# Expert weights relaid in device memory and fetched by GpSimd only where the expert changes

## The chip, the cores and the metric

The kernel runs on one core of a Trainium2 chip. The metric is the time of one execution on the device, in microseconds (us). The core has five engines that run side by side and meet at semaphores: TensorE (PE in the profile; its weight loads are PEld), VectorE (DVE), ScalarE (ACT), GpSimd (POOL) and SyncE (SP), which here only issues DMAs. Sixteen DMA engines move data between device memory and the on-chip memory of 128 partitions. A difference of less than about 0.2% can't be told from none.

## The reference

Two layers over a graph of 2,500 nodes with 1,024 features and 40,000 edges. Each layer is a graph convolution followed by a feed-forward block, both added to `x`. The part that matters here is the last block, a mixture of eight experts of which each node uses two:

```python
router_probs = softmax(flat @ router_w + router_b)          # [2500, 8]
topk_probs, topk_idx = top_k(router_probs, 2)
h1 = gelu(einsum('td,edh->teh', flat, rw1) + rb1)           # rw1: [8, 1024, 256]
expert_out = einsum('teh,ehd->ted', h1, rw2) + rb2          # rw2: [8, 256, 1024]
mixed = einsum('ted,te->td', expert_out, weights)           # weights: top 2 only
```

Before it stands the second graph layer, with attention: every edge gets a score from its two nodes, and rows of the projected nodes are summed with those scores.

## The kernel before

The program is a row of stages, each with its own block of five instruction streams; a stage starts when the one before has ended on all engines. The stages that the change touches are three.

**Attention** (`stage_attention`, about 1428 to 2050 us). SP loads the weight matrix W in eight pieces of 512 KB (line 1032). TensorE computes the scores of all nodes; when they are all kept, SP stores the source half as rows in device memory (line 1034, 40 KB, `el`). GpSimd then gathers a row per edge, 352 DMAs of 128 rows (line 1051), while TensorE computes the projected rows. TensorE has 160 products to do before it needs the first 32 gathers (`Z_FIRST`); from then on the order of products and score chunks is written out by `attention_turns`. All of SP's DMAs go through one queue, in order.

**Routing** (`stage_route`, about 3052 to 3106 us). The 5,000 places (2,500 nodes, two experts each) are sorted by expert into 28 groups of 256 (`PG`), each group with one expert. Each expert's part is padded to whole groups, and groups past the end get the last expert. `group_expert` holds the expert of each group.

**Experts** (`stage_experts`, about 3106 to 3580 us). For each group SP reads the group's expert into a register and loads the two weight matrices, 1 MB each, into one buffer each (`raw1`, `raw2`, both `e_raw` in the profile; lines 1978 and 1981), as soon as VectorE has freed it. ScalarE casts them to a high part (`e_w_hi`), VectorE subtracts to get the low part (`e_w_lo`) and frees the buffer. GpSimd gathers the 256 rows of the group in two DMAs (line 1995), TensorE turns them (`e_turned`), ScalarE and VectorE split them (`e_hi`, `e_lo`), TensorE computes the hidden layer in 48 products (`e_hidden`), ScalarE the Gelu (`e_act_out`), VectorE splits it (`e_h_hi`, `e_h_lo`), TensorE computes the output in 24 products (`e_y`), VectorE adds the bias, ScalarE scales, and GpSimd adds the rows to the output in device memory with two scatters (line 2005); each pair of scatters waits until the pair before has landed.

The stage is a software pipeline written out in full (`in_turn`): in step s every engine works on groups s, s-1 and s-2, in the order of its `body`. ScalarE in step s does: the two casts of turned rows of group s-1, the two casts of the weights of group s, the Gelu of group s-1, the scaling of group s-2. VectorE: `e_lo` of s-1 and output sums of s-2 in turn, the two weight subtractions of s, `e_h_hi` and `e_h_lo` of s-1. GpSimd: the gathers of s, then the scatters of s-2. ScalarE and VectorE begin the stage with a wait for all three bias loads (`small_in`), of which the last is a broadcast of 4 MB (`e_all_bias`, line 1984).

Of the kernel before, what the change touches and what calls it, by code (L numbers as in the profile page):

```python
# [6 lines left out]
I32 = mybir.dt.int32  # L7
U32 = mybir.dt.uint32
ALU = mybir.AluOpType
ACT = mybir.ActivationFunctionType  # L10
AX = mybir.AxisListType
P = 128
N_NODES = 2500
N_EDGES = 40000
D = 1024
KD = D // P
# [16 lines left out]
EXPERTS = 8  # L33
# [961 lines left out]
def stage_attention(nc, g):  # L995
    with ExitStack() as ctx:
# [19 lines left out]
        stored = [sem(f"stored{k}") for k in range(2)]  # L1016
# [12 lines left out]
        def _(sp):  # L1029
            for c in range(KD):  # L1030
                at_least(sp, w_low, c - 1)
                sp.dma_start(zout[:, c % 2, :].rearrange("p (h f) -> p h f", h=HEADS), w_rows[c]).then_inc(w_in[c % 2], 16)
            sp.wait_ge(scores_kept, NT)
# [4 lines left out]
            for k in range(2):  # L1038
                sp.wait_ge(stored[k], 16 * (NT // 2))

# [704 lines left out]
def stage_route(nc, g):  # L1745
    with ExitStack() as ctx:
# [26 lines left out]
        group_count = sb("group_count", [P, PG])  # L1773
# [13 lines left out]
        def _(pool):  # L1787
# [7 lines left out]
            q.iota(iota_g[:], pattern=[[GT * P, PG]], base=0, channel_multiplier=0, **small)  # L1795
            q.memset(ones[:], 1.0)
# [33 lines left out]
        def _(dve):  # L1830
# [99 lines left out]
            st.done(v.tensor_scalar(g.expert[:], group_count[:], float(EXPERTS - 1), None, ALU.min))  # L1930

# [13 lines left out]
def stage_experts(nc, g):  # L1945
    with ExitStack() as ctx:
# [14 lines left out]
                 "hi_ready lo_ready hidden_ready act_ready split_ready y_ready y_kept y_scaled bias1_ready").split()  # L1961
# [7 lines left out]
        def _(sp):  # L1969
# [5 lines left out]
            for i in range(PG):  # L1975
                e = sp.value_load(g.expert[0:1, i:i + 1], min_val=0, max_val=EXPERTS - 1)
                at_least(sp, m.raw1_used, i)
                sp.dma_start(raw1[:].rearrange("p (c f) -> p c f", c=KD),
                             g.rw1.rearrange("e (c p) f -> p (e c) f", p=P)[:, bass.ds(e * KD, KD), :]).then_inc(m.raw1_in, 16)
                at_least(sp, m.raw2_used, i)  # L1980
                sp.dma_start(raw2[:].rearrange("p (m n) -> p m n", m=2),
                             g.rw2.rearrange("e (m p) n -> p (e m) n", p=P)[:, bass.ds(e * 2, 2), :]).then_inc(m.raw2_in, 16)
                if i == 0:
                    sp.dma_start(all_bias2[:], g.rb2.rearrange("e d -> (e d)").partition_broadcast(P)).then_inc(m.small_in, 16)

        @block.gpsimd
        def _(pool):
            def body(item):
# [11 lines left out]
                if it:  # L2000
                    for q in range(GT):
# [5 lines left out]
                            in_=y_out[:, it.i % 2, q, :], in_offset=None, compute_op=ALU.add).then_inc(y_added, 16)  # L2007
# [198 lines left out]
```

## Time and profile before

| | us |
|---|---|
| median of three runs | 3577.93 |
| lowest, highest | 3573.08, 3578.49 |
| profiled execution, its own time | 3581.93 |
| its span | 3580.2 |
| TensorE busy over the span | 2847.5 (80%) |
| VectorE busy | 2455.1 (69%) |
| GpSimd busy | 1714.2 (48%) |
| ScalarE busy | 1536.9 (43%) |

The span is the stretch that the profiler recorded; the time of the same execution is 1.7 us longer. Busy shares are averages over stages with different limits, and a change in one stage is judged by what that stage waits for. In the profile a row of engines reads: where, engine, operation, output<-inputs, shape, how often, and in brackets the idle time before it with the instruction that ended it.

### The profile page before, as it was taken

The numbers are of one execution on the slowest core, as the hardware profiler recorded it, in microseconds if no ns is written. First come the engines' busy times: TensorE is split into PE (matmuls) and PEld (weight loads), VectorE is DVE, ScalarE is ACT, GpSimd is POOL, SyncE is SP. The second block draws the span as 40 slices with busy tenths as digits, with TensorE's granted clock in tenths as the row PEclk, the third lists the DMA queues.
The fourth block names the chain that finished last, engine by engine and source line by source line (L and its number), as shares of the span: only waits on it lengthen the run. The fifth ranks groups of instructions, "written<-read, shape, count | busy, mean of one in ns | idle before, by whom it ended". The sixth has DMA issues, their size and how long they took to land. (4 is left out here: it accounts for less than half of the span.)

```text
span 3580.2 us, 50457 instructions
## 1 busy us (share of the span) xinstructions
PE 2847.5 (80%) x13602; PEld 2228.0 (62%) x13602; DVE 2455.1 (69%) x5351; ACT 1536.9 (43%) x3068; POOL 1714.2 (48%) x1564
## 2 busy tenths in 40 slices
PE   0996102999996777889899899999999699289996
PEld 0885101444443665877777588888887688278886
DVE  6222602999997665527777799999999564467774
ACT  1221000333333765523333377777776332055554
POOL 4777873666664221247777344444443111023332
PEclk9998555999998898579999899999999688599999
DMA  3333306999997011101111188887877332289997
GB/s 103 79 96 109 92 2 246 353 349 351 348 347 225 30 41 55 40 20 20 26 20 26 38 263 259 262 261 260 260 261 230 114 139 106 103 239 284 282 284 181
DMA packets 223841, 609.09 MB, mean 170 GB/s; under 512 B 47387, under 2 KB 85650, under 8 KB 223582
## 3 DMA queue, kind: packets, MB, share of 16 engines
q0 software_dynamic: 139008, 429.63, 38.7%
q1 hardware_dynamic: 84702, 177.85, 14.5%
q8 instruction: 65, 1.06, 0.1%
q14 instruction: 66, 0.54, 0.1%
HBM read 521.91 MB, written 85.11 MB: 170 GB/s over the span
## 5 line engine op out<-in xcount | busy, mean ns | idle before, releaser
L640 POOL DMA_INDIRECT g_rows<-z_rows,edge_src x704 | 700.4, 995 | 615.6 <-PE g_totals L1397 307.8
L705 PE MATMUL g_sums<-g_rows,g_share 128*128 128x512 f32 x704 | 333.0, 595 | 211.3 <-DVE g_goes L746 211.3
L483 POOL DMA_INDIRECT edge_list<-payload,row_i x320 | 402.3, 1257 | 144.1 <-issue 141.3
L691 ACT ACTIVATE g_scaled_hi<-g_rows,edge_weight_sorted 128x1024 fp32r<-128x1024 f32 x176 | 202.6, 1151 | 540.6 <-DMA g_rows<-z_rows,edge_src 505.4
L1051 POOL DMA_INDIRECT shared<-el_rows,edge_src x352 | 334.8, 951 | 178.8 <-issue 107.0
L1390 PE MATMUL g_sums<-g_rows,g_share 128*128 128x256 f32 x1408 | 348.9, 391 | 0.0
L705 PEld LDWEIGHTS g_sums<-g_rows,g_share 128*128 128x128 f32 x704 | 133.5, 190 | 312.3 <-DVE g_goes L746 211.7
L1342 ACT ACTIVATE g_scaled_hi<-g_rows,g_factor 128x256 fp32r<-128x256 f32 x704 | 299.9, 496 | 4.3 <-DMA g_rows<-z_rows,edge_src 3.2
L1466 DVE SCALAR_TENSOR_TENSOR g_scaled_lo<-g_rows,g_factor,g_scaled_hi 128x256 fp32r<-128x256 f32 x704 | 293.4, 479 | 1.1 <-ACT g_scaled_hi L1342 0.9
L1390 PEld LDWEIGHTS g_sums<-g_rows,g_share 128*128 128x128 f32 x1408 | 255.6, 191 | 27.6
L1245 DVE TENSOR_REDUCE t_largest<-t_masked 128x4 f32<-128x512 f32 x352 | 231.9, 685 | 55.7 <-PE t_masked L1117 49.4
L728 DVE SCALAR_TENSOR_TENSOR g_scaled_lo<-g_rows,edge_weight_sorted,g_scaled_hi 128x1024 fp32r<-128x1024 f32 x176 | 225.9, 1283 | 41.5 <-ACT g_scaled_hi L691 39.6
L2005 POOL DMA_INDIRECT out_dram<-e_y_out,sorted_token x56 | 89.3, 1594 | 270.4 <-ACT e_y_out L2082 255.7
L1428 DVE TENSOR_TENSOR x_all<-x_all,g_sums 128x1024 f32 x176 | 213.9, 1216 | 0.0
L738 DVE TENSOR_TENSOR x_all<-x_all,g_sums 128x1024 f32 x176 | 213.3, 1212 | 0.4 <-PE g_sums L710 0.2
L710 PE MATMUL g_sums<-g_scaled_hi,g_goes 128*128 128x512 f32 x352 | 159.4, 453 | 33.8 <-DVE g_scaled_lo L728 33.1
L710 PEld LDWEIGHTS g_sums<-g_scaled_hi,g_goes 128*128 128x128 f32 x352 | 66.1, 188 | 172.4 <-DVE g_scaled_lo L728 163.3
L1167 ACT ACTIVATE t_apart<-iota,t_minus_place 128x128 fp32r<-128x128 f32 x352 | 125.9, 397 | 109.0 <-PE t_masked L1117 108.1
L1115 PE MATMUL t_masked<-t_never,t_apart 128*128 128x512 f32 x352 | 149.1, 423 | 23.2 <-DVE t_largest L1245 14.3
L1475 DVE TENSOR_TENSOR e_w_lo<-e_raw,e_w_hi 128x2048 fp32r<-128x2048 f32 x56 | 125.8, 2285 | 30.0 <-ACT e_w_hi L2061 28.5
L1579 POOL TENSOR_TENSOR x_all<-x_all,s_bias 128x1024 f32<-128x1024 f32 (+1 forms) x20 | 46.7, 2356 | 207.2 <-ACT s_rows L1651 207.2
L1117 PE MATMUL t_masked<-t_el_rows,t_pick 128*128 128x512 f32 x352 | 144.3, 410 | 0.0
(359 smaller groups left out, 7696.5 us busy)
## 6 DMA issues: line engine op xcount, KB each, us to landing
e_raw<-in_L_ffn_rw_dram SPq DMA_DIRECT2D x56, 1024.0 KB, 7.5
g_rows<-z_rows,edge_src POOLq DMA_INDIRECT x704, 5.7
z_rows<-z_zout SPq DMA_DIRECT2D x20, 512.0 KB, 2.9
x_rows<-x_all SPq DMA_DIRECT2D x20, 512.0 KB, 2.7
z_rows<-t_zout SPq DMA_DIRECT2D x20, 512.0 KB, 2.8
s_x<-x_rows SPq DMA_DIRECT2D x10, 1024.0 KB, 8.9
xn_rows<-s_rows SPq DMA_DIRECT2D x10, 1024.0 KB, 4.1
z_x<-in_x_dram SPq DMA_DIRECT2D x19, 512.0 KB
```

The costliest lines, as they stand in the source:

```text
L483: pool.indirect_dma_start(out=g.lists[k], out_offset=bass.IndirectOffsetOnAxis(ap=row_i[0:EP, c:c + 1], axis=0), in_=payload[0:EP, c, :], ...
L640: pool.indirect_dma_start(out=r.rows[:, slot, :], out_offset=None, in_=table, in_offset=bass.IndirectOffsetOnAxis(ap=g.src[:, i * GT + q:i ...
L705: nc.tensor.matmul(sums[:, k, h, :], share[:, k, :], r.rows[:, k * GT, h * HALF:(h + 1) * HALF], start=True, stop=False)
L710: mm = nc.tensor.matmul(sums[:, k, h, :], goes[:, k, :], part[:, m, h * HALF:(h + 1) * HALF], start=False, stop=n == 1)
L728: v.scalar_tensor_tensor(out=scaled_lo[:, m, :], in0=r.rows[:, k * GT + 1, :], scalar=g.weight[:, bass.ds(it.i * GT + 1, 1)], in1=scaled_h ...
L738: v.tensor_tensor(to, to, sums[:, it.buf(4)].rearrange("p h n -> p (h n)"), ALU.add).then_inc(added, 1)
L1051: pool.indirect_dma_start(out=g.edge_el[:, n, :], out_offset=None, in_=g.el, in_offset=bass.IndirectOffsetOnAxis(ap=g.src[:, n:n + 1], axi ...
L1245: v.tensor_reduce(largest[:, q, :], masked[:, n % 3, :].rearrange("p (h n) -> p h n", h=HEADS), AX.X, ALU.max).then_inc(taken, 1)
L1342: ins = s.activation(scaled_hi[:, m, cols], r.rows[:, k * GT + 1, cols], ACT.Copy, scale=factor[:, k, 1, h:h + 1])
L1390: t.matmul(sums[:, m, h // 2, h % 2 * HF:(h % 2 + 1) * HF], share[:, m, h, :], r.rows[:, k * GT, h * HF:(h + 1) * HF], start=False, stop=F ...
L1428: v.tensor_tensor(to, to, sums[:, m].rearrange("p h n -> p (h n)"), ALU.add).then_inc(added, 1)
L1466: ins = v.scalar_tensor_tensor(out=scaled_lo[:, m, cols], in0=r.rows[:, k * GT + 1, cols], scalar=factor[:, k, 1, h:h + 1], in1=scaled_hi[ ...
```

## The change

Two tables are added in device memory, `w1_rows` and `w2_rows`, each of 1,024 rows of 8 KB: row e*128+p holds what partition p needs of expert e, in one run. In the attention stage SP copies the sixteen matrices from the inputs into them, memory to memory, behind the loads of W and ahead of the store of the score rows. Routing computes `weight_row`, for each group and partition the row of the table, with 1,024 added where the group has the same expert as the group before: such a row is out of bounds, and the fetch leaves it out. In the expert stage the weights are fetched by GpSimd as indirect DMAs, group 0's ahead of everything and group i+1's at the end of step i, behind the gathers and scatters of that step. SP is left with the bias loads. The 4 MB bias has a semaphore of its own (`bias2_in`), for which only VectorE waits, before its first output sum. The casts and subtractions are done for every group as before.

```diff
--- before.py
+++ after.py
@@ -1013,7 +1013,7 @@
         masked, row_bank = a.psum("t_masked", [P, 3, HALF]), a.psum("t_row_bank", [P, HALF])
         w_in = [sem(f"w_in{k}") for k in range(2)]
         el_in = [sem(f"el_in{b}") for b in range(NB)]
-        stored = [sem(f"stored{k}") for k in range(2)]
+        stored, relaid = [sem(f"stored{k}") for k in range(2)], sem("relaid")
         (w_high, w_low, mv_ready, std_ready, rstd_ready, xn_ready, turned_ready, hi_ready, lo_ready, scores_ready,
          scores_kept, el_stored, apart_ready, pick_ready, parts_ready, rows_turned, rows_ready, masked_ready,
          taken, z_ready, z_kept, v_done) = (sem(n) for n in (
@@ -1030,6 +1030,11 @@
             for c in range(KD):
                 at_least(sp, w_low, c - 1)
                 sp.dma_start(zout[:, c % 2, :].rearrange("p (h f) -> p h f", h=HEADS), w_rows[c]).then_inc(w_in[c % 2], 16)
+            for e in range(EXPERTS):
+                sp.dma_start(g.w1_rows[e * P:(e + 1) * P, :].rearrange("p (c f) -> p c f", c=KD),
+                             g.rw1[e].rearrange("(c p) f -> p c f", p=P)).then_inc(relaid, 16)
+                sp.dma_start(g.w2_rows[e * P:(e + 1) * P, :].rearrange("p (m n) -> p m n", m=2),
+                             g.rw2[e].rearrange("(m p) n -> p m n", p=P)).then_inc(relaid, 16)
             sp.wait_ge(scores_kept, NT)
             sp.dma_start(g.el.rearrange("(t p) h -> p t h", p=P), g.scores[:, :, 0:HEADS]).then_inc(el_stored, 16)
             for t in range(NT):
@@ -1037,6 +1042,7 @@
                 sp.dma_start(g.z1[t * P:(t + 1) * P, :], zout[:, t % 2, :]).then_inc(stored[t % 2], 16)
             for k in range(2):
                 sp.wait_ge(stored[k], 16 * (NT // 2))
+            sp.wait_ge(relaid, 16 * 2 * EXPERTS)
 
         @block.gpsimd
         def _(pool):
@@ -1770,7 +1776,8 @@
         late, member = sb("late", [P, EXPERTS, TOPK, NEAR]), sb("member", [P, EXPERTS, NEAR])
         spare, spare_place, fits = (sb(n, [P, EXPERTS, NEAR]) for n in ("spare", "spare_place", "fits"))
         of_group = sb("of_group", [P, PG, EXPERTS])
-        group_count = sb("group_count", [P, PG])
+        group_count, row_of = sb("group_count", [P, PG]), sb("row_of", [P, PG])
+        repeats, partition = sb("repeats", [P, PG]), sb("partition", [P, 1])
         at_row, at_col = sb("at_row", [P, ALL, P], F32R), sb("at_col", [P, ALL, 3, PT], F32R)
         is_col = sb("is_col", [P, ALL, PT])
         held, empty = sb("held", [P, PT]), sb("empty", [P, PT])
@@ -1793,6 +1800,8 @@
             q.iota(iota_r[:], pattern=[[1, P]], base=0, channel_multiplier=0, **small)
             q.iota(iota_c[:], pattern=[[1, PT]], base=0, channel_multiplier=0, **small)
             q.iota(iota_g[:], pattern=[[GT * P, PG]], base=0, channel_multiplier=0, **small)
+            q.iota(partition[:], pattern=[[0, 1]], base=0, channel_multiplier=1, **small)
+            q.memset(repeats[:], 0.0)
             q.memset(ones[:], 1.0)
             q.memset(none[:], 0.0)
             q.memset(place_i[:], PT * P)
@@ -1928,6 +1937,11 @@
                                 ALU.is_equal).then_inc(rows_ready, 1)
             st.link(v.tensor_reduce(group_count[:], of_group[:], AX.X, ALU.add))
             st.done(v.tensor_scalar(g.expert[:], group_count[:], float(EXPERTS - 1), None, ALU.min))
+            st.link(v.tensor_scalar(group_count[:], group_count[:], float(EXPERTS - 1), None, ALU.min))
+            st.done(v.tensor_tensor(repeats[:, 1:PG], group_count[:, 1:PG], group_count[:, 0:PG - 1], ALU.is_equal))
+            st.link(v.tensor_scalar(row_of[:], group_count[:], float(P), partition[:, 0:1], ALU.mult, ALU.add))
+            st.done(v.scalar_tensor_tensor(out=g.weight_row[:], in0=repeats[:], scalar=float(EXPERTS * P), in1=row_of[:],
+                                           op0=ALU.mult, op1=ALU.add))
 
             dve.wait_ge(pairs_sorted, 1)
             st.link(v.tensor_copy(held[:], sorted_pairs[:, 0:PT]))
@@ -1958,7 +1972,7 @@
         turned, y = a.psum("e_turned", [P, 2, HALF]), a.psum("e_y", [P, GT, 2, HALF])
         hidden = a.psum("e_hidden", [P, HALF])
         names = ("small_in raw1_in raw2_in raw1_used raw2_used w1_high w2_high v_done turned_ready "
-                 "hi_ready lo_ready hidden_ready act_ready split_ready y_ready y_kept y_scaled bias1_ready").split()
+                 "hi_ready lo_ready hidden_ready act_ready split_ready y_ready y_kept y_scaled bias1_ready bias2_in").split()
         m = Named(**{n: a.sem(f"e_{n}") for n in names})
         gathered = [[a.sem(f"e_gathered{k}{q}") for q in range(GT)] for k in range(2)]
         y_added = a.sem("e_y_added")
@@ -1972,19 +1986,21 @@
                     sp.dma_start(all_bias1[:].rearrange("p (e m) -> p m e", m=2)[:, c, :],
                                  g.rb1.rearrange("e (m p) -> m p e", p=P)[c]).then_inc(m.small_in, 16)
 
-            for i in range(PG):
-                e = sp.value_load(g.expert[0:1, i:i + 1], min_val=0, max_val=EXPERTS - 1)
-                at_least(sp, m.raw1_used, i)
-                sp.dma_start(raw1[:].rearrange("p (c f) -> p c f", c=KD),
-                             g.rw1.rearrange("e (c p) f -> p (e c) f", p=P)[:, bass.ds(e * KD, KD), :]).then_inc(m.raw1_in, 16)
-                at_least(sp, m.raw2_used, i)
-                sp.dma_start(raw2[:].rearrange("p (m n) -> p m n", m=2),
-                             g.rw2.rearrange("e (m p) n -> p (e m) n", p=P)[:, bass.ds(e * 2, 2), :]).then_inc(m.raw2_in, 16)
-                if i == 0:
-                    sp.dma_start(all_bias2[:], g.rb2.rearrange("e d -> (e d)").partition_broadcast(P)).then_inc(m.small_in, 16)
+            sp.dma_start(all_bias2[:], g.rb2.rearrange("e d -> (e d)").partition_broadcast(P)).then_inc(m.bias2_in, 16)
 
         @block.gpsimd
         def _(pool):
+            def weights(i):
+                for raw, table, used, arrived in ((raw1, g.w1_rows, m.raw1_used, m.raw1_in),
+                                                  (raw2, g.w2_rows, m.raw2_used, m.raw2_in)):
+                    at_least(pool, used, i)
+                    pool.indirect_dma_start(
+                        out=raw[:], out_offset=None, in_=table,
+                        in_offset=bass.IndirectOffsetOnAxis(ap=g.weight_row[:, i:i + 1], axis=0),
+                        bounds_check=EXPERTS * P - 1, oob_is_err=False).then_inc(arrived, 16)
+
+            weights(0)
+
             def body(item):
                 it = item(0)
                 if it:
@@ -2005,6 +2021,9 @@
                         pool.indirect_dma_start(
                             out=g.out, out_offset=bass.IndirectOffsetOnAxis(ap=g.sorted_token[:, n:n + 1], axis=0),
                             in_=y_out[:, it.i % 2, q, :], in_offset=None, compute_op=ALU.add).then_inc(y_added, 16)
+                it = item(0)
+                if it and it.i + 1 < PG:
+                    weights(it.i + 1)
             in_turn(PG, body, 2)
             pool.wait_ge(y_added, 16 * PT)
 
@@ -2043,7 +2062,7 @@
         @block.scalar
         def _(act):
             s = nc.scalar
-            act.wait_ge(m.small_in, 48)
+            act.wait_ge(m.small_in, 32)
 
             def body(item):
                 for q in range(GT):
@@ -2087,7 +2106,6 @@
         def _(dve):
             v = nc.vector
             st = Steps(dve, m.v_done)
-            dve.wait_ge(m.small_in, 48)
 
             def body(item):
                 for q in range(GT):
@@ -2104,6 +2122,8 @@
                         if q == 0:
                             e = dve.value_load(g.expert[0:1, it.i:it.i + 1], min_val=0, max_val=EXPERTS - 1)
                             shift = all_bias2[:, bass.ds(e * D, D)]
+                        if n == 0:
+                            dve.wait_ge(m.bias2_in, 16)
                         dve.wait_ge(m.y_ready, n + 1)
                         at_least(dve, y_added, (it.i - 1) * GT * 16)
                         v.tensor_tensor(y_out[:, k, q, :], y[:, q].rearrange("p h n -> p (h n)"), shift,
@@ -2140,6 +2160,7 @@
         sw1=sw1, sb1=sb1, sw2=sw2, sb2=sb2, rw1=rw1, rb1=rb1, rw2=rw2, rb2=rb2, out=out,
         lists=[scratch(f"edge_list{k}", [P * NE, 4]) for k in range(LISTS)],
         z0=scratch("z0_rows", [NPAD, D]), z1=scratch("z1_rows", [NPAD, D]), el=scratch("el_rows", [NPAD, 4]),
+        w1_rows=scratch("w1_rows", [EXPERTS * P, KD * EH]), w2_rows=scratch("w2_rows", [EXPERTS * P, 2 * D]),
         x2=scratch("x2_rows", [NPAD, D]), xn3=scratch("xn3_rows", [NPAD, D]),
     )
     with ExitStack() as ctx:
@@ -2168,6 +2189,7 @@
         g.logits = a.sb("logits", [P, NT, EXPERTS])
         g.sorted_prob = a.sb("sorted_prob", [P, PT])
         g.expert = a.sb("group_expert", [P, PG], I32)
+        g.weight_row = a.sb("weight_row", [P, PG], I32)
         g.sorted_token = a.sb("sorted_token", [P, PT], I32)
         with nc.sbuf_tensor("x_all", [P, NT, D], F32) as x_all:
             g.x_all = x_all
```

SP's queue in the attention stage, before (W load, score rows, projected rows, end of the stage, next loads):

```order
L1028 UNCONDITIONAL_BRANCH
L1032 DMA t_zout<-in_L_gnn_W_dram 128x4x256 x8
L1034 DMA el_rows<-shared 128x20x4
L1037 DMA z_rows<-t_zout 128x1024 x20
L996 UNCONDITIONAL_BRANCH
```

and in the difference between the two programs at that place:

```order
 L1032 DMA t_zout<-in_L_gnn_W_dram 128x4x256 x8
-L1034 DMA el_rows<-shared 128x20x4
-L1037 DMA z_rows<-t_zout 128x1024 x20
+L1034 DMA w_rows<-in_L_ffn_rw_dram 1024x1x256
+L1036 DMA w_rows<-in_L_ffn_rw_dram 256x1x1024
...
+L1039 DMA el_rows<-shared 128x20x4
+L1042 DMA z_rows<-t_zout 128x1024 x20
```

The pair of `w_rows` copies stands eight times, once for each expert, and the store of the score rows comes after all sixteen.

GpSimd's stream at the start of the expert stage, before (the loop is written out, so that each step stands by itself; `e_rows` is a gather of rows, `out_dram` a scatter):

```order
L1986 UNCONDITIONAL_BRANCH
L1995 DMA e_rows<-xn_rows,sorted_token 128x1024 x6
L2005 DMA out_dram<-e_y_out,sorted_token 2500x1024 x2
L1995 DMA e_rows<-xn_rows,sorted_token 128x1024 x2
L2005 DMA out_dram<-e_y_out,sorted_token 2500x1024 x2
```

and now (`e_raw` is a fetch of weights):

```order
L1991 UNCONDITIONAL_BRANCH
L1997 DMA e_raw<-w_rows,weight_row 128x2048 x2
L2011 DMA e_rows<-xn_rows,sorted_token 128x1024 x2
L1997 DMA e_raw<-w_rows,weight_row 128x2048 x2
L2011 DMA e_rows<-xn_rows,sorted_token 128x1024 x2
L1997 DMA e_raw<-w_rows,weight_row 128x2048 x2
L2011 DMA e_rows<-xn_rows,sorted_token 128x1024 x2
L2021 DMA out_dram<-e_y_out,sorted_token 2500x1024 x2
L1997 DMA e_raw<-w_rows,weight_row 128x2048 x2
L2011 DMA e_rows<-xn_rows,sorted_token 128x1024 x2
L2021 DMA out_dram<-e_y_out,sorted_token 2500x1024 x2
```

From the fourth group on, its weights stand behind the scatters of an earlier group and ahead of its own gathers. On SP's stream the 56 weight loads and the register reads between them are gone; what is left of the stage there is this:

```order
L1504 UNCONDITIONAL_BRANCH
L1982 UNCONDITIONAL_BRANCH
L1986 DMA e_all_bias<-in_L_ffn_rb_dram 128x8x1 x2
L1989 DMA e_all_bias<-in_L_ffn_rb_dram 128x8192
L1960 UNCONDITIONAL_BRANCH
```

The bias broadcast no longer has the first group's weights ahead of it on that queue. TensorE's and ScalarE's instructions stand as before.

## Rows read from the trace of the kernel before

**Rows 1.** Chain that ended last, from 3050 us: start, length (us), what.
```profile
3109.97 21.66 DMA e_all_bias<-in_L_ffn_rb_dram
...
3143.77 7.33 PE e_hidden L253 x48
...
3346.49 1.62 POOL out_dram L2005
...
3361.37 1.61 POOL out_dram L2005
```

**Rows 2.** Waits from 3100 to 3580 us: us in total, times, longest.
```profile
PE e_y L253 <- DVE e_h_lo L1475: 34.9, 28, 2.1
```

**Rows 3.** Stretches: us, busy (x) by engine, PEclk, DMA share, GB/s.
```profile
core 0: us, PE busy (x) PEld busy (x) DVE busy (x) ACT busy (x) POOL busy (x), PEclk, DMA share, GB/s
1478.00:1553.70 75.70, 67.44 (x314) 66.32 (x315) 38.07 (x98) 32.15 (x37) 4.72 (x2) 0.50 0.03 8
...
3120.00:3126.00 6.00, 0.00 (x0) 0.00 (x0) 0.00 (x0) 0.00 (x0) 0.00 (x0) 0.50 1.09 465
...
3138.40:3141.00 2.60, 1.53 (x8) 1.56 (x8) 0.92 (x1) 0.00 (x0) 0.00 (x0) 0.50 1.05 362
...
3300.00:3520.00 220.00, 200.73 (x1295) 175.77 (x1294) 153.60 (x119) 129.30 (x135) 77.31 (x60) 1.00 0.98 283
```

**Rows 4.** ScalarE in order of time, head and one later period of the stage.
```profile
3131.66 1.90 ACT L2061 CAST e_w_hi<-e_raw 128x2048 fp32r<-128x2048 f32 x1 [76.21 <-DMA e_all_bias<-in_L_ffn_rb_dram]
...
3135.26 1.00 ACT L2054 CAST e_hi<-e_turned 128x1024 fp32r<-128x1024 f32 x1
...
3351.57 1.91 ACT L2061 CAST e_w_hi<-e_raw 128x2048 fp32r<-128x2048 f32 x1
...
3359.22 0.84 ACT L2075 ACTIVATE e_act_out<-e_hidden,e_bias 128x256 f32<-128x256 f32 x2 [3.70 <-PE e_hidden L253]
```

**Rows 5.** VectorE in order of time, the same period.
```profile
3354.60 4.49 DVE L1475 TENSOR_TENSOR e_w_lo<-e_raw,e_w_hi 128x2048 fp32r<-128x2048 f32 x2
3360.09 0.43 DVE L2127 CAST e_h_hi<-e_act_out 128x512 fp32r<-128x512 f32 x1 [1.00 <-ACT e_act_out L2075]
```

**Rows 6.** GpSimd in order of time, the same period.
```profile
3348.41 1.58 POOL L2005 DMA_INDIRECT out_dram<-e_y_out,sorted_token  x1 [0.30 <-issue]
3350.30 0.99 POOL L1995 DMA_INDIRECT e_rows<-xn_rows,sorted_token  x1 [0.30 <-issue]
3351.60 0.97 POOL L1995 DMA_INDIRECT e_rows<-xn_rows,sorted_token  x1 [0.30 <-issue]
```

**Rows 7.** SP's queue in order of time, the same period.
```profile
3342.18 0.37 SPq L1978 DMA_DIRECT2D e_raw<-in_L_ffn_rw_dram  x1
```

**Rows 8.** DMA issues of the whole trace: last number is median us to landing.
```profile
shared<-el_rows,edge_src POOLq DMA_INDIRECT x352, 2.4
...
e_rows<-xn_rows,sorted_token POOLq DMA_INDIRECT x56, 7.8
```

**Rows 9.** Tile `e_raw`: landing of its 56 loads.
```profile
DMA to landing us min/median/max: 6.0/7.5/12.4
```

**Rows 10.** SP's queue in order of time, attention stage.
```profile
1427.87 50.16 SPq L1032 DMA_DIRECT2D t_zout<-in_L_gnn_W_dram  x8
1553.67 0.37 SPq L1034 DMA_DIRECT2D el_rows<-shared  x1
```

**Rows 11.** GpSimd in order of time, attention stage.
```profile
1561.18 0.98 POOL L1051 DMA_INDIRECT shared<-el_rows,edge_src  x1 [71.82 <-DMA el_rows<-shared]
```

**Rows 12.** VectorE in order of time, attention stage and end of routing.
```profile
1602.53 0.27 DVE L1238 CAST t_el_parts<-shared 128x128 fp32r<-128x128 f32 x1 [8.66 <-DMA shared<-el_rows,edge_src]
...
3104.53 0.22 DVE L1933 COPY r_held<-r_sorted_pairs 128x56 f32<-128x56 f32 x1 [6.12 <-PE r_sorted_pairs L1825]
```

**Rows 13.** TensorE in order of time, attention stage.
```profile
1603.27 0.63 PE L1105 MATMUL t_row_bank<-ident,t_el_parts 128*64 128x128 f32 x4 [3.93 <-DVE t_el_parts L1239]
```

**Rows 14.** GpSimd in order of time, start of routing.
```profile
3053.32 0.15 POOL L1795 IOTA r_iota_g<- 128x28 f32 x1
```

**Rows 15.** DMA issues from 3566 to 3567 us: median us to landing.
```profile
out_dram<-e_y_out,sorted_token POOLq DMA_INDIRECT x1, 6.7
```

## The prediction, made before the changed kernel ran

> **What bounds the kernel now.** I read the chain that ended last first, because the change touches three stages and only the chain says which of their waits reach the end. From 3,167 us on it repeats one pattern, a scatter issued by GpSimd every 14.88 us (3346.49, 3361.37) [rows 1]: the period of one group in the expert stage. It does not vary, although DMA is busy 98% of the stage at 283 GB/s [rows 3], and a period that constant is set by an engine. TensorE is busy 200.73 of 220.00 us there, 13.6 of each 14.88, at full granted clock [rows 3]. What it lacks is mainly the wait for `e_h_lo`, made by VectorE: 34.9 us in 28 times, 1.25 us a group [rows 2]. So the 56 MB of weights are fetched beside other work, and a smaller fetch by itself gives nothing. What matters is when the weights are in. Their slack is read in one period. ScalarE casts them from 3351.57 on (twice 1.91 us) and later sits idle 3.70 us before the Gelu at 3359.22 [rows 4]. VectorE subtracts twice from 3354.60 to 3359.09 and is idle only 1.00 us before `e_h_hi` at 3360.09 [rows 5]. VectorE is the narrow place.
>
> At the head of the stage it is otherwise. ScalarE starts only at 3131.66, when the 4 MB bias broadcast has landed, issued at 3109.97 behind 2 MB of weights; the first product of the hidden layer starts at 3143.77 [rows 1, 4].
>
> The third place is the attention stage. SP issues the last W load at 1478.0 and then nothing until the store of the score rows at 1553.67 [rows 10]. GpSimd's gathers wait for that store until 1561.18 [rows 11], VectorE waits 8.66 us for the first 32 of them, and TensorE, out of products at 1599.3, waits 3.93 us for VectorE's parts [rows 12, 13]. A later store would go straight to TensorE.
>
> **The change, part by part.** The sum is made against the profiled execution's own 3581.93 us (span 3580.2 and 1.7 around it). The median of the runs is 3577.93, 4.0 less, and I take those 4.0 off at the end.
>
> *Routing.* One iota and one memset on GpSimd stand ahead of the semaphore for which VectorE waits: twice some 0.15 us [rows 14], +0.3. The four new VectorE operations, about 1 us, stand where VectorE is idle for 6.12 us until TensorE has sorted [rows 12]: nothing; 1 us is their price without that cover.
>
> *Relaying in the attention stage.* Sixteen copies of 1 MB, 16.8 MB from memory to memory, go on SP's queue between the last W load and the store of the score rows. The gap is 75.7 us with DMA busy 3% [rows 3], so they cost TensorE nothing directly, only through what is queued behind them: the store, and with it 352 gathers. No row shows a copy from memory to memory. If a byte costs once, as in a load, 16.8 MB at 362 GB/s [rows 3] take 46 us and fit: 0. If both sides are paid, 33.6 MB take 93 us at 362 GB/s and 72 at the 465 of the broadcast [rows 3]; counted from 1480 the end is 1552 to 1573, up to 19 us behind the store's issue. The loads touch memory once and these twice, so I take the second, in its middle: +10. Each us stays, since the gathers (1.26 us apart, 40 us for 32) hardly outrun TensorE afterwards. The ends are 0 and 25. The Trainium skill (DMA: Bandwidth & Descriptors, Latency and other measured facts) gives 207 to 214 GB/s per direction for large copies between memory tensors; by it the copies would take some 80 us and the store would be 6 us late. No run here shows it yet.
>
> *Head of the expert stage.* The bias now gates only VectorE's first output sum, long after. The weights of group 0 go first on GpSimd's queue, at 3107.5, the bias beside them on SP's. A weight load beside much other traffic landed in up to 12.4 us [rows 9]; the same puts these at 3120 and the row gathers behind them at 3125 to 3128. The work from the first cast of turned rows (3135.26) to the hidden layer (3143.77) took 8.5 us [rows 1, 4], so that starts at 3133.5 to 3136.5 instead of 3143.77. I take -10, with the ends -6 (the bias's 32 KB rows get more than their share) and -14 (weights in at 3114).
>
> *The loop, a group whose expert repeats.* The reference's router gives 153, 31, 227, 2276, 48, 1570, 220 and 475 places to the eight experts. That is 23 groups of 256, padded to 28 with the last expert: 8 fetches (groups 0, 1, 2, 3, 12, 13, 20, 21) and 20 repeats. SP issued weights as soon as VectorE had freed the buffer, at 3342.18 [rows 7]. Now GpSimd issues them after the scaling of the group before last and its two scatters, where row gathers stood, at 3350.30 and 3351.60 [rows 6]. That is 8 us later and 1.3 us before ScalarE wants them, for a DMA that has a semaphore even if it moves nothing. Its landing time is in no row. From below it is 2.4 us, that of the small gathers, from above 7.8, a row gather's under load [rows 8]. It stands in GpSimd's queue behind the scatter of 3348.41 [rows 6]; a scatter with the queues nearly empty lands 6.7 us after its issue [rows 15], here at 3355.1. I take that moment, 4.8 us. Then ScalarE casts to 3357.0, VectorE's two subtractions (4.49) end at 3361.6, and `e_h_hi` is 1.5 us late. As the next fetch goes out in a period that is longer too, half stays: 0.75 us each, 15 us for 20. At 3.3 us or less the price would be 0, at 7.8 it would be 2.2 each. The Trainium skill (DMA: Bandwidth & Descriptors, Queues, rings and completion order) says that a semaphore's increment lands after all earlier writes of the same DMA engine. By it even an empty fetch isn't seen before the scatter ahead of it, and without it these 15 us would be 0.
>
> *The loop, a group with a new expert.* Groups 1 and 2 come in while the pipeline fills; from 3 on the fetch stands behind a scatter, five times. The least that a weight load took is 6.0 us [rows 9]; behind a scatter I take 7 for the first MB, 3357.3, and 3 more for the second (1.05 MB at 362 GB/s), 3360.3. A cast of 1.92 and a subtraction of 2.24 end at 3364.5, 4.4 us late. Little of it comes back: 3.6 each, 18 us, with the ends 2.5 and 6 each. The row gathers, now behind 2 MB, land near 3363, still ahead of `e_h_lo`.
>
> *What is removed.* DMA load halves in most groups, but TensorE waits for no transfer in the loop: 0. Its granted clock stayed at the 2.4 GHz level with waits of 1.25 us [rows 2, 3], and I expect the same with 2.
>
> Sum: 3581.93 + 0.3 + 10 - 10 + 15 + 18 = 3615.2; less 4.0: **3611**.
>
> **Rivals.** *A, empty fetches are seen at once.* The repeats cost 0, the new experts 3 each, 15 in all. For it: 2.4 us for small gathers [rows 8]. Against: those have no scatter ahead of them. 3577.9 + 0.3 + 10 - 10 + 15 = 3593.
>
> *B, faster: with less in its queues DMA runs everywhere at the rate of the broadcast,* 465 GB/s [rows 3]. The relay then ends at 1552, before the store; the head gives 14; empty fetches come within 3.3 us, and new experts cost 1 us beyond the slack, five times: 3577.9 + 0.3 - 14 + 5 = 3569. It decides once relay and loop together cost under 14 us. For it: the load of 98% falls to half. Against: 1 MB behind a scatter has never landed within 3.3 us.
>
> *C, relaying is slow.* The first matrix is copied in rows of 1 KB, with both sides in memory. At half the rate for that matrix (93 us for it, 46 for the other) the copies take 140 us, the store is 65 us late, and TensorE waits for all of it: 3577.9 + 0.3 + 65 - 10 + 33 = 3666. For it: no row shows such copies. Against: 1 KB rows load at 362 GB/s.
>
> *D, skipping does not skip.* If every group fetched its 2 MB, 25 groups would cost 3.6 each: 3577.9 + 0.3 + 10 - 10 + 90 = 3668. Nothing in the trace speaks for it, and nothing there shows a skipped row.
>
> **Chances.** The forecast 0.50, A 0.17, B 0.17, C 0.11, D 0.05. The forecast's own range is 3593 to 3635. The range given takes in B's upper part and C's lower: 3571 to 3652. A difference of 0.2% (7 us) is about what can be told from no change. Faster by more is most of B, 0.12; within it the rest of B and the edge of A, 0.09; slower 0.79.
>
> **What would show it.** The scatters come 15.6 us apart in groups 5 to 11, some 18.5 at 12, 13, 20 and 21. ScalarE's cast of the first weight has idle time before it that the fetch ends; it has none now [rows 4]. TensorE's wait for `e_h_lo` grows from 34.9 to near 68 us. The score gathers start near 1571 instead of 1561. The first hidden product comes some 10 us nearer to the end of routing. The forecast is wrong if the period stays 14.88 in the repeats (A or B), if it is over 17 (D), or if the score gathers start after 1590 (C).

## The result, and the profile after

The changed kernel takes 3632.36 us (median of 4 runs, 3632.31 to 3634.06) against 3578.21 us before (3573.08 to 3578.56), a ratio of 1.0156 with a 95% interval from 1.0138 to 1.0173. It is slower by 54 us; 33 were forecast, and 3632 lies inside the range of 3571 to 3652. The profiled execution took 3632.34 us, its span is 3630.5 us, 50.3 us more than before. (In later comparisons the kernel before had medians of 3577 to 3580 us; each kernel is compared with the runs of before on its own chip.)

The span splits at two events of the expert stage. GpSimd's first DMA of the stage starts at 3102.83 instead of 3107.53; in kernels that are the same ahead of it this moment lay between 3098 and 3109, so these 4.7 us are no effect. From there to the first hidden product it was 36.2 us (3107.53 to 3143.77, the latter in [rows 1]) and is 27.5: 8.7 won. From there to the end it was 436.4 and is 500.2: 63.7 lost. The first hidden product now, on TensorE in order of time:

```profile
3130.33 0.58 PE L253 MATMUL e_hidden<-e_hi,e_w_hi 128*128 128x256 f32 x1 [2.36 <-DVE e_lo L2116]
```

The attention stage paid nothing. SP in order of time: the copies stand one behind the other, and SP is held at them, but the last is issued at 1520.04 and done being issued at 1524.8, 28 us ahead of the store that answers to [rows 10]:

```profile
1477.51 0.68 SPq L1034 DMA_DIRECT2D w_rows<-in_L_ffn_rw_dram  x1
...
1520.04 4.72 SPq L1036 DMA_DIRECT2D w_rows<-in_L_ffn_rw_dram  x1
1553.13 0.38 SPq L1039 DMA_DIRECT2D el_rows<-shared  x1
```

and GpSimd's score gathers start at 1560.11, where it was 1561.18 [rows 11]. The stretches of that time (columns as in [rows 3]) give the rate of the copies:

```profile
1478.00:1500.00 22.00, 19.26 (x91) 18.89 (x90) 11.50 (x31) 11.87 (x14) 4.69 (x2) 0.50 0.96 317
1500.00:1525.00 25.00, 22.26 (x105) 21.89 (x105) 14.04 (x34) 10.38 (x13) 0.00 (x0) 0.50 1.00 333
```

In the loop the chain that ended last no longer has one period. These are the first scatters of groups 5 to 11. A group's scatters go out two steps behind its own, so the last two stand in the steps that bring in the new experts of groups 12 and 13, and the others in steps with an expert that repeats: 17.71, 15.22, 17.78, 15.58, 18.96 and 19.14 us apart, for 14.88 before [rows 1].

```profile
3242.36 0.83 POOL out_dram L2021
...
3260.07 0.83 POOL out_dram L2021
...
3275.29 0.83 POOL out_dram L2021
...
3293.07 0.83 POOL out_dram L2021
...
3308.65 0.83 POOL out_dram L2021
...
3327.61 0.83 POOL out_dram L2021
...
3346.75 0.83 POOL out_dram L2021
```

The waits of the stage name the way. ScalarE waits for weights before nearly every first cast, which it did once before and for the bias [rows 4] (the longest of the 27, 67.2 us, is the one ahead of the stage; the 26 in the loop sum to 87.4); the last row answers to [rows 2], 34.9 us:

```profile
ACT e_w_hi L2080 <- DMA e_raw<-w_rows,weight_row: 154.6, 27, 67.2
...
PE e_y L253 <- DVE e_h_lo L1481: 66.0, 28, 4.6
```

One period of ScalarE, VectorE and TensorE shows it link by link. GpSimd has two scatters at 3260.07 and 3261.99 and then the fetch, which moves nothing, at 3263.86:

```profile
3261.99 1.57 POOL L2021 DMA_INDIRECT out_dram<-e_y_out,sorted_token  x1 [0.30 <-issue]
3263.86 1.06 POOL L1997 DMA_INDIRECT e_raw<-w_rows,weight_row  x1 [0.30 <-issue]
```

In the chain, in order of time, the second of these scatters lands at 3269.01:

```profile
3261.99 7.02 DMA out_dram<-e_y_out,sorted_token
```

ScalarE sees the fetch 0.21 us after that, 5.36 us after its issue, having idled 3.96, and has no slack left before the Gelu (3.70 us in [rows 4]):

```profile
3269.22 1.91 ACT L2080 CAST e_w_hi<-e_raw 128x2048 fp32r<-128x2048 f32 x1 [3.96 <-DMA e_raw<-w_rows,weight_row]
...
3273.14 0.84 ACT L2094 ACTIVATE e_act_out<-e_hidden,e_bias 128x256 f32<-128x256 f32 x2
```

In each of the 20 groups with a repeated expert the first cast starts 0.18 to 0.24 us after the second scatter ahead of the fetch has landed. This is the plainest sign in the trace that the empty fetch's semaphore stands behind that scatter.

VectorE's subtractions end at 3275.73, so `e_h_hi` follows them without idle time, 1.7 us after the Gelu ended at 3273.98 (compare [rows 5]):

```profile
3271.23 4.50 DVE L1481 TENSOR_TENSOR e_w_lo<-e_raw,e_w_hi 128x2048 fp32r<-128x2048 f32 x2 [2.96 <-ACT e_w_hi L2080]
3275.64 0.42 DVE L2147 CAST e_h_hi<-e_act_out 128x512 fp32r<-128x512 f32 x1
```

TensorE waits 3.21 us, and soon after its products take 0.63 us each instead of 0.40 and follow each other after 0.43 us instead of 0.23:

```profile
3276.84 0.50 PE L253 MATMUL e_y<-e_w_hi,e_h_hi 128*128 128x512 f32 x1 [3.21 <-DVE e_h_lo L1481]
...
3279.11 0.63 PE L253 MATMUL e_y<-e_w_lo,e_h_hi 128*128 128x512 f32 x1
```

The reason for the last is in the stretches: the granted clock is at its full level of 2.4 GHz through the wait and at half, 1.2 GHz, soon after it, for some 3.3 us.

```profile
3276.00:3277.00 1.00, 0.16 (x1) 0.16 (x2) 0.77 (x3) 0.95 (x2) 1.00 (x1) 1.00 0.00 0
3277.00:3278.00 1.00, 1.00 (x5) 0.82 (x6) 1.00 (x1) 0.00 (x0) 0.69 (x2) 0.96 0.77 66
3278.00:3281.00 3.00, 3.00 (x9) 2.35 (x8) 0.21 (x1) 0.00 (x0) 2.39 (x3) 0.50 0.92 161
```

The length of one wait does not settle it. Ten of the 28 waits for `e_h_lo` are of 3.02 to 4.62 us; near eight of them the clock was at half, but it stayed full behind those of 3.07 us (ended at 3381.53) and 3.30 us (3556.04). It was at half for some 3 us behind waits of only 1.94 us (3571.35) and 2.09 us (3588.36) too. Two stretches, behind the wait of 3.30 and behind that of 2.09:

```profile
3556.04:3560.00 3.96, 3.96 (x21) 3.38 (x22) 1.97 (x2) 0.11 (x1) 3.04 (x4) 1.00 0.83 123
...
3589.40:3591.40 2.00, 2.00 (x7) 1.52 (x6) 1.11 (x1) 0.00 (x0) 1.57 (x1) 0.50 0.93 117
```

A long wait in one period and a short one in the next make the alternation. How one leads to the other is argued, not shown: in the slowed period everything that TensorE releases is later, the weights are in time again, and the wait after it is short. Over the whole loop, before and after, the granted clock fell from 0.98 to 0.91:

```profile
3144.00:3580.00 436.00, 379.61 (x2448) 333.59 (x2448) 285.12 (x220) 236.34 (x249) 138.33 (x106) 0.98 0.90 256
```
```profile
3130.00:3630.00 500.00, 405.35 (x2448) 356.26 (x2448) 286.28 (x221) 238.46 (x249) 197.06 (x160) 0.91 0.60 143
```

These two rows also split the 64 us on TensorE. The same 2,448 products keep it busy for 405.35 us instead of 379.61, 25.7 more, at the lower clock. Its idle time grows by 38.3 us, of which the waits for `e_h_lo` are 31.1 (66.0 for 34.9). This is bookkeeping and not yet cause: without the lower clock the waits would have been other ones.

### The profile page after: what moved, and what is told of

Same layout as the page of the kernel before. It is cut to its first block and busy times, and to the rows that moved or that the text cites. A ratio compares the mean times of both kernels' runs of the same rounds, so it can differ in the third digit from the quotient of the medians.

```text
span 3630.5 us, 50340 instructions
## 1 busy us (share of the span) xinstructions
PE 2866.9 (79%) x13602; PEld 2244.8 (62%) x13602; DVE 2457.5 (68%) x5355; ACT 1538.4 (42%) x3068; POOL 1775.7 (49%) x1622
## 5 line engine op out<-in xcount | busy, mean ns | idle before, releaser
L253 PE MATMUL e_y<-e_w_hi,e_h_hi 128*128 128x512 f32 x224 | 105.0, 469 | 66.0 <-DVE e_h_lo L1481 66.0
```

## The experiments

**The place in GpSimd's queue.** The fetch is moved ahead of the scatters of its step.

```diff
@@ stage_experts, body of GpSimd @@
+                it = item(0)
+                if it and it.i + 1 < PG:
+                    weights(it.i + 1)
                 it = item(2)
                 if it:
                     ... (the two scatters)
-                it = item(0)
-                if it and it.i + 1 < PG:
-                    weights(it.i + 1)
```

> The changed kernel with one thing moved: in each step GpSimd issues the next group's weights ahead of the two scatters instead of behind them. Theory (the place in GpSimd's queue): the fetch then waits only for VectorE's subtractions of the step, goes out some 4 us earlier and has no scatter ahead of it, so ScalarE no longer waits for it; the period returns to 14.9 us in every group, TensorE's waits for e_h_lo to near 35 us in all, and the 64 us that the loop lost are back: 3565 to 3572. Rival (a fetch by GpSimd is slow wherever it stands, by its own latency and by what it takes from the scatters in the same queue): the period stays at 16 or more and the time over 3600.

Measured: 3569.77 us (median of 10 runs), ratio to before 0.9977 (0.9965 to 0.9989). The theory holds, the rival falls. GpSimd in one period:

```profile
3313.84 1.11 POOL L1997 DMA_INDIRECT e_raw<-w_rows,weight_row  x1 [0.31 <-issue]
3315.25 1.62 POOL L2024 DMA_INDIRECT out_dram<-e_y_out,sorted_token  x1 [0.30 <-issue]
...
3330.14 1.62 POOL L2024 DMA_INDIRECT out_dram<-e_y_out,sorted_token  x1 [0.30 <-issue]
```

The period is 14.88 us again (3315.25 to 3330.14), in all groups but one (15.3), and so the 64 us of the loop are all due to where the fetch stood: from the first hidden product to the end it is 436.9 us, for 436.4 before. GpSimd now waits for VectorE's subtractions in each step, in time that it has.

**Bytes.** Every group fetches its 2 MB, at the changed kernel's place and then at the early place; the edit is the same.

```diff
-                                           scalar=float(EXPERTS * P), in1=row_of[:],
+                                           scalar=0.0, in1=row_of[:],
```

> The changed kernel, but every group fetches its 2 MB, repeated or not. Theory: a repeat costs less than a new expert only by the time of the bytes; the 20 repeats, at a mean period of 16.7 us, go to the 18.7 to 19.1 us of the groups with a new expert: +40 us, near 3673. Rival (what costs is the late semaphore alone, bytes are hidden): no change, 3632.

Measured: 3698.3 us, ratio 1.0340 (1.0323 to 1.0357), 66 us over the changed kernel; the periods are 18.6 to 20.5 us throughout. The direction was right, the size too small: 20 groups cost 3.3 us more each, not 2. At this place leaving out repeats is worth a good deal.

> The kernel of the first experiment (weights ahead of the scatters), but every group fetches its 2 MB. Theory (the loss was the place, not the bytes): at this place there is room for the bytes too, and TensorE sets the period; at most the row gathers, now behind 2 MB more, come late by 0 to 1 us in a group: 3570 to 3590. Rival (leaving repeated experts out is what makes the early place work): near e2's period of 19.6, over 3650.

Measured: 3575.18 us, ratio 0.9994 (0.9983 to 1.0006). At the early place the same bytes cost 5 to 6 us over e1 by the medians and the ratios, and the two intervals just touch. In the profiled execution it is 11 us, in five periods of 16.7 to 17.1 us and two of 15.4, in which TensorE waited for row gathers behind the weights. That leaving out 20 of 28 fetches pays depends on the place as well.

**No byte moves in the loop.** Only group 0 fetches.

```diff
-            st.done(v.tensor_tensor(repeats[:, 1:PG], group_count[:, 1:PG], group_count[:, 0:PG - 1], ALU.is_equal))
+            st.done(v.memset(repeats[:, 1:PG], 1.0))
```

> The changed kernel, but only group 0 fetches weights; all later groups leave the fetch out and compute with the first expert's weights. Theory: the groups 3, 12, 13, 20 and 21 lose the bytes, some 2 us each beyond a repeat, and groups 1 and 2 a little: 3632 less 12 to 18, 3614 to 3620; the loss of the repeats, over 30 us, stays, though no byte of weights moves in the loop. Rival (the loss comes from moving weights through GpSimd's queue): with no bytes the period is 14.9 and the time near 3570.

Measured: 3623.59 us, ratio 1.0121 (1.0105 to 1.0138). That is 9 us under the changed kernel by the medians and 12 by the ratios, at or below the low end of the 12 to 18 expected. The rival falls plainly: some 44 of the 54 us are lost without a byte of weights in the loop. The periods still alternate, 15.0 to 18.9.

**How long an empty fetch takes.** Three small gathers stand in place of the two scatters.

```diff
-                        pool.indirect_dma_start(out=g.out, ..., compute_op=ALU.add).then_inc(y_added, 16)
+                    for q in range(3):
+                        n = it.i * 3 + q
+                        pool.indirect_dma_start(out=g.edge_el[:, n, :], in_=g.el, ...
+                            ).then_inc(y_added if q < GT else spare_added, 16)
```

> The changed kernel with its two scatters a group replaced by three small gathers (128 rows of 16 bytes, about the same time on GpSimd), so that the fetch is issued at the same place with nothing long ahead of it; the output sums are left out. It measures how long an empty fetch takes to be seen. Theory (its semaphore stands behind the scatter): without one ScalarE sees it 2.4 us after the issue, and waits about 1 us or not at all before its first weight cast, and the period is under 15.2. Rival (an empty fetch takes 5.4 us by itself): ScalarE waits 4 us as now and the period stays near 16.6.

Measured: 3597.17 us, one run, with a profile. GpSimd issues a repeated group's fetch and ScalarE sees it 2.14 us later:

```profile
3242.29 1.00 POOL L1998 DMA_INDIRECT e_raw<-w_rows,weight_row  x1 [0.30 <-issue]
```
```profile
3244.43 1.91 ACT L2085 CAST e_w_hi<-e_raw 128x2048 fp32r<-128x2048 f32 x1 [2.29 <-DMA e_raw<-w_rows,weight_row]
```

In 19 of the 20 repeats it was 2.12 to 2.23 us, against 5.1 to 6.8 behind a scatter in the changed kernel. The periods away from new experts are 14.9 but for two of 15.2 and 15.3. So an empty fetch is cheap by itself. This kernel also moves fewer bytes, as its scatters are gone, so alone it can't tell a semaphore that stands behind the scatter from queues that are less full; the landings read above, 0.18 to 0.24 us ahead of the cast in all 20 groups, speak for the first. With a new expert the first MB was seen after 5.6 to 5.9 us (8.1 to 9.1 behind scatters), and the eight periods at new experts and right behind them were still 17.1 to 19.3, 27 us over 14.9 in all, for 32 in the changed kernel. For these groups the bytes alone, issued so late, cost nearly as much.

**The clock's share.** Seven products on TensorE fill its wait for `e_h_lo`.

```diff
+FILL = 7
...
-                        pe.wait_ge(m.split_ready, it.i + 1)
                         pe.wait_ge(m.raw2_used, it.i + 1)
                         at_least(pe, m.y_kept, it.i * GT + q - 1)
+                        if q == 0:
+                            for f in range(FILL):
+                                t.matmul(y[:, 0, 0, :], w2_hi[:, k, 0, 0:P], w2_hi[:, k, 0, 0:HALF], start=True, stop=True)
+                        pe.wait_ge(m.split_ready, it.i + 1)
```

> The changed kernel with seven products of 128x512 added on TensorE in each group, on data that is there, into a bank that the next product overwrites, ahead of the wait for e_h_lo: 1.6 us of work in the time in which TensorE waited 3 us or more. Theory (a good part of the loss is the granted clock, which falls to half for 3.3 us after a wait of 3.2 us; by the rows it takes some 30 us): the clock stays up, the periods of 17.7 us shorten to near 16, and the kernel gets faster by 15 to 30 us though it does more work: 3600 to 3617. Rival (the clock costs nothing beside the late weights): the added work costs 0 to 10 us, 3632 to 3642.

Measured: 3621.4 us (3616.61 to 3628.92), ratio 1.0128 (1.0105 to 1.0151), 11 us under the changed kernel by the medians and 10 by the ratios, with 196 products more. The ratio's interval overlaps that of the changed kernel (1.0138 to 1.0173), so the gain as a number is at the edge of the noise. The direction is the theory's; the size is under its 15 to 30. The periods of the repeats no longer alternate and lie near 16.1 (15.6 to 17.1), and the granted clock over the loop is 0.97:

```profile
3128.00:3615.00 487.00, 424.11 (x2633) 372.83 (x2632) 284.72 (x220) 236.57 (x248) 197.85 (x160) 0.97 0.61 145
```

So the rival's 3632 to 3642 did not come, and the fall of the clock costs about 10 us net, an estimate from these two kernels. What is plain in the trace is the other part: with the clock kept up the alternation is gone. The late weights are then felt in every period instead, a likely reason why not more comes back; the filling may cost something too, above all around new experts, where periods of 19 to 21 remain. Neither was tried alone.

**The copies alone.** The kernel before with the sixteen copies and the wait for them, and nothing else.

> The kernel before with the sixteen copies added in the attention stage and nothing else. In the changed kernel's trace the last copy is issued at 1520 and the score gathers start 1.1 us earlier than before, so the theory is now: no cost, 3576 to 3582. The theory on record (copies paid on both sides end behind the store's issue) would give 3588.

Measured: 3574.5 us, ratio 0.9996 (0.9984 to 1.0007). The copies are free; the term of +10 was wrong.

**The head alone.** The kernel before, with the bias on its own semaphore.

```diff
-                    ... rb2 ... .partition_broadcast(P)).then_inc(m.small_in, 16)
+                    ... rb2 ... .partition_broadcast(P)).then_inc(m.bias2_in, 16)
-            act.wait_ge(m.small_in, 48)
+            act.wait_ge(m.small_in, 32)
-            dve.wait_ge(m.small_in, 48)
+                        if n == 0:
+                            dve.wait_ge(m.bias2_in, 16)
```

> The kernel before with one part of the change alone: the 4 MB bias broadcast has its own semaphore, for which only VectorE waits, before its first output sum; weights come from SP as before. Theory: ScalarE starts when the first weights have landed, near 3120 instead of 3131.7, and the first hidden product 9 to 12 us earlier, while the period stays 14.88: 3566 to 3569. Rival (the gain at the head is given back, since the weights of group 1 or the gathers come no earlier): 3575 to 3578.

Measured: 3573.47 us, ratio 0.9978 (0.9968 to 0.9987). The first hidden product comes 23.8 us after the stage's first DMA, for 36.2, and the period stays 14.9. By the profile that is 12 us; the ratio gives 5 to 11. Part was given back, as the rival said, though not all: the weights of group 1 now travel beside the broadcast, ScalarE waits 5.59 us for them, and TensorE after that for `e_h_lo`:

```profile
3146.76 0.79 PE L253 MATMUL e_y<-e_w_hi,e_h_hi 128*128 128x512 f32 x1 [5.25 <-DVE e_h_lo L1475]
```

This kernel is as fast as e1, which has the relaid weights and the fetch by GpSimd besides. What e1 wins over the kernel before is thus the head; the rest of the change brings nothing that these runs can tell.

**The bias later still.** Two kernels in which the broadcast no longer travels beside the first weights.

```diff
-                if i == 0:
+                if i == 1:
                     sp.dma_start(all_bias2[:], ...)
```

> The kernel before, with the bias broadcast on its own semaphore as in e4_bias_apart and also issued later, behind the weights of group 1. Theory (all that the change gains is the head, where 4 MB of bias travel beside the first weights): the first weights land near 8 us instead of 11 us after the stage starts and the first hidden product comes 21 us instead of 24 us after it; period 14.88 as before: 14 to 16 us under before, 3561 to 3566. Rival (the broadcast then delays the weights of group 1, for which ScalarE waits behind the turned rows): no better than e4, 0.998 of before.

Measured: 3565.49 us, ratio 0.9964 (0.9950 to 0.9977), the lowest of all, though its interval overlaps those of e1 and e4. ScalarE's first weight cast starts at 3109.53, 10.4 us after the stage's first DMA, and the first hidden product at 3122.98, 23.8 after it, the same as in e4. The first weights gained next to nothing by having the broadcast out of their way. What came better is behind them: with the weights of group 1 ahead of the broadcast TensorE's wait there is the usual one,

```profile
3132.59 0.50 PE L253 MATMUL e_y<-e_w_hi,e_h_hi 128*128 128x512 f32 x1 [1.24 <-DVE e_h_lo L1475]
```

and the first scatter comes 48.1 us after the stage's first DMA, for 54.0 in e4. The number of the expectation, 3561 to 3566, was met by another way than it said, and so by luck; against its own before it is 12 us and not 14 to 16.

For the kernel of e1 the wait `sp.wait_ge(m.raw2_in, 16)` was put ahead of the broadcast.

> The kernel of e1_fetch_first (weights by GpSimd ahead of the scatters), with the bias broadcast issued by SP only when the weights of group 0 are in. Theory: the first weights land 6 us instead of 16 us after the start of the stage, the rows near 12 us, and the first hidden product 20 to 22 us after it instead of 28.5; period 14.88: 6 to 8 us under e1, 3561 to 3565. Rival (the gathers, not the bias, are late at the head): within 2 us of e1.

Measured: 3568.44 us, ratio 0.9974 (0.9962 to 0.9985), not told apart from e1: the theory's 3561 to 3565 was missed. The rival had the number, within 2 us of e1, but not the reason, since the first hidden product came at 19.6 us instead of 28.5. Most was given back: the weights of group 1 now travel beside the broadcast, and ScalarE waits for them.

```profile
3126.46 1.91 ACT L2081 CAST e_w_hi<-e_raw 128x2048 fp32r<-128x2048 f32 x1 [7.21 <-DMA e_raw<-w_rows,weight_row]
```

## Why the prediction was right, and where not

The direction, the place and the chain were right: the loop, a late fetch behind two scatters, ScalarE, VectorE's second subtraction, `e_h_lo`, TensorE. e1 shows the place; e7 and the landings of the scatters show what the semaphore stands behind. In spans it lost 50.3 us where 33.3 were forecast, or 55 without the 4.7 by which the stage happened to start earlier. That the forecast was no further off is in part luck: the +10 for the relay was wrong, and without it the other terms give 23. The terms, one by one:

*Routing, +0.3:* not visible. *The relay, +10:* 0, by e8, and the score gathers started at 1560 and not near 1571. The step that failed was "the loads touch memory once and these twice, so I take the second": the copies ran at 317 to 333 GB/s in the column in which loads run at 362, and took some 53 us of a gap of 75.7, so the first reading, a byte that costs once, was near. The Trainium skill (DMA: Bandwidth & Descriptors, Latency and other measured facts) has 207 to 214 GB/s per direction for copies between memory tensors in tiles of 128 x 16 KiB, at the better row pitches; ours are of another shape, the trace shows more, and it decides. *The head, -10:* -8.7. By the prediction's own 3133.5 to 3136.5 for the first hidden product it was 7 to 10, and -10 was its far end.

*Repeats, +15:* the periods away from new experts sum to 30 us over 14.9, 16.6 in the mean where 15.6 was forecast. Two things were wrong. The fetch was seen 5.1 to 6.8 us after its issue, not 4.8: the 6.7 us of a scatter had been read with the queues nearly empty [rows 15]. By the prediction's own rule 5.7 gives (5.7 - 3.3) / 2 = 1.2 us each, 24 us. The other step that failed is "Its granted clock stayed at the 2.4 GHz level with waits of 1.25 us [rows 2, 3], and I expect the same with 2". The waits for `e_h_lo` came to 66.0 us where near 68 were forecast, so their sum was right; but the clock fell, at eight of the ten waits of 3 us and more and at some of 2, and the same products took 25.7 us more, a term that the sum did not have. e6 puts what the clock costs net at about 10 us, so the two do not simply add up: the slowed period seems to give the next fetch its time back. The Trainium skill (DMA: Bandwidth & Descriptors, Queues, rings and completion order) says, in its paragraph on the queues of SP and ScalarE, that the increment lands after the earlier writes of the same DMA engine. The traces of GpSimd's fetches agree: 2.14 us without and 5.1 to 6.8 with a scatter ahead, and in the latter case 0.18 to 0.24 us behind its landing.

*New experts, +18:* 32 us, with 25 of it at groups 12, 13, 20 and 21 and 7 where group 3 comes in. The first MB was seen after 8.1 to 9.1 us where 7 had been taken, and a late fetch lengthens the period behind it too: 18.96, 19.14 and then 18.15 at groups 12 and 13, and 19.15, 20.41 and then 18.3 at 20 and 21. The prediction had priced one period each, near 18.5.

Of the rivals, A is refuted by 5.1 us and more for empty fetches; B was right that the relay costs nothing and in no other part, as its copies would have taken 72 us at 465 GB/s with both sides counted, and took some 53; C and D are refuted by e8 and by e2, which is 66 us slower.

## What to carry to other kernels

Bytes that are hidden are worth little when taken away: at the early place 20 fetches of 2 MB left out were worth 5 to 6 us of 3,575. What counts is where an instruction stands in its queue, what it waits for there, and what its semaphore stands behind. An indirect DMA that skips all its rows is still a DMA, whose semaphore queues behind a scatter issued before it; put such a fetch ahead of the long DMA of its step. Where TensorE is the bound, price a new wait by its single cases and not by the mean, and look at the granted clock around each, since it may stay down after the wait is over. And try the parts of a change alone: all that this one won came with a semaphore of its own for one bias, as far as these runs can tell.

## What was not expected of the hardware

- Copies from memory to memory ran nearly as fast as loads: 317 to 333 GB/s, with rows of 1 and 4 KB. SP was held at them, 4.7 to 7.3 us at every second one, so a queue of large copies also blocks the engine that issues it.
- An indirect DMA with all rows out of bounds is seen 2.14 us after its issue with only small gathers ahead (e7), and 0.2 us behind the landing of the scatter where one stands ahead, 5.1 to 6.8 us after its issue. GpSimd spends 1.0 us on it, as on one that moves 1 MB.
- Behind the wait of 3.21 us TensorE's granted clock was still full for 1.1 us and then at half for some 3.3 us, while TensorE was busy. In the loop of before, with waits of 1.24 us, it stayed full [rows 2, 3], and also behind the one of 2.12 us at its end; in the changed kernel it fell behind waits of 1.94 and 2.09 us and did not behind those of 3.07 and 3.30. No single wait's length decides it in these traces.
- A loop can settle in two alternating periods, here 15.2 and 17.8 us, though the fetch is late in each. The mean (16.6) hides both. With TensorE's wait filled (e6) and the clock at 0.97 it settled at 16.1 instead.
- What stays open is how the 64 us divide by cause between lateness and clock, as e6 changes both. By TensorE's time it is 25.7 us of slower products and 38.3 of idle time.
